# Self-attention: the weighting of a period in two halves of 256 columns, one behind each of the first two scores

## What is computed

```python
def _mha(q_in, kv_in, in_w, in_b, out_w, out_b):
    ...
    scores = jnp.einsum('bhqd,bhkd->bhqk', q, k) / jnp.sqrt(jnp.float32(dh))
    attn = jax.nn.softmax(scores, axis=-1)
    out = jnp.einsum('bhqk,bhkd->bhqd', attn, v)
    out = out.transpose(0, 2, 1, 3).reshape(q_in.shape[0], q_in.shape[1], D)
    return out @ out_w.T + out_b
...
q = _ln(latents, sa_ln_g, sa_ln_b)
x = latents + _mha(q, q, sa_in_w, sa_in_b, sa_out_w, sa_out_b)
```

## Time and profile before

| | |
|---|---|
| median of three runs | 1690.89 us |
| profiled execution | 1686.37 us, span of the trace 1684.6 us |
| TensorE busy in the span | 1441.5 us (86%) |
| VectorE busy in the span | 1181.5 us (70%) |
| ACT busy in the span | 844.1 us (50%) |
| self-attention, first to last score | 173 to 818 us |

### The profile page before, as it was taken

One profiled execution on the slowest core, in us unless ns is written; L12 is line 12 of the kernel. 1 busy time (PEld: TensorE's weight loads), 2 busy tenths in 40 slices (PEclk: granted clock), 3 DMA queues, 4 the chain that ended last, 5 costly groups with the idle time before them and its releaser, 6 DMA issues. The chain is left out here.

```text
span 1684.6 us, 29075 instructions
## 1 busy us (share of the span) xinstructions
PE 1441.5 (86%) x9973; PEld 745.6 (44%) x9974; DVE 1181.5 (70%) x1725; ACT 844.1 (50%) x1709; POOL 743.7 (44%) x465
## 2 busy tenths in 40 slices
PE   5993999999999999999658888873299999999996
PEld 3550222222222222222233544442288888888885
DVE  4755999999999999997165777434655665655653
ACT  2330788888888888888414545340022222222221
POOL 1003999999930000000131221100158887888884
PEclk8995899999999999999876979565599999999999
DMA  3556645574522111200264665535722332333331
GB/s 119 188 212 177 163 132 153 156 215 134 157 57 84 32 32 33 84 1 2 89 142 105 163 140 98 121 73 191 297 42 55 56 55 48 53 60 54 54 57 16
DMA packets 134790, 172.68 MB, mean 103 GB/s; under 512 B 30008, under 2 KB 100089, under 8 KB 134187
## 3 DMA queue, kind: packets, MB, share of 16 engines
q1 hardware_dynamic: 107499, 119.26, 26.6%
q0 software_dynamic: 27200, 52.24, 12.9%
HBM read 102.09 MB, written 66.25 MB: 100 GB/s over the span
## 5 line engine op out<-in xcount | busy, mean ns | idle before, releaser
L1093 DVE TENSOR_REDUCE sa_half_maxs<-sa_psm 128x2 f32<-128x1024 f32 x512 | 604.7, 1221 | 49.7 <-PE sa_psm L961 41.2
L1077 ACT ACTIVATE sa_p<-sa_pss 128x512 f32<-128x512 f32 x1024 | 533.0, 603 | 89.8 <-PE sa_pss L1004 89.6
L1004 PE MATMUL sa_pss<-sa_q,sa_k 49*128 49x512 f16 x1024 | 312.2, 385 | 7.8
L1019 PE MATMUL sa_pso<-sa_p,sa_v 128*32 128x512 f32 x2048 | 273.8, 606 | 18.8 <-ACT sa_o L1055 9.4
L961 PE MATMUL sa_psm<-sa_k,sa_q 48*128 48x512 f16 x1024 | 260.9, 395 | 30.5 <-DMA sa_k<-dram_sa_qk_parts 19.2
L2295 ACT ACTIVATE moe_h<-moe_psh,moe_b 128x256 f32<-128x256 f32 x312 | 122.4, 475 | 328.4 <-PE moe_psh L2232 328.4
L1004 PEld LDWEIGHTS sa_pss<-sa_q,sa_k 49*128 49x128 f16 x1024 | 77.7, 94 | 320.2 <-ACT sa_p L1077 264.9
L1366 POOL TENSOR_TENSOR x_xb<-x_xb,early_bo 128x1024 f32<-128x1024 f32 x4 | 9.4, 2350 | 373.4 <-DMA x_xb<-in_x 373.4
L2231 PE MATMUL moe_psh<-moe_hl,w_high 128*128 128x256 f16 x624 | 171.0, 274 | 0.0
L2230 PE MATMUL moe_psh<-moe_hh,w_high 128*128 128x256 f16 x624 | 170.9, 274 | 0.0
L2232 PE MATMUL moe_psh<-moe_hh,w_low 128*128 128x256 f16 x624 | 170.9, 274 | 0.0
(11 more groups left out here) (205 smaller groups left out, 2026.2 us busy)
## 6 DMA issues: line engine op xcount, KB each, us to landing
sa_w_stage<-in_w POOLq DMA_DIRECT2D x32, 512.0 KB, 5.3
dram_sa_v<-qkv_v_sb SPq DMA_DIRECT2D x8, 1024.0 KB, 5.0
dram_sa_qk_parts<-qkv_part SPq DMA_DIRECT2D x16, 512.0 KB, 6.0
sa_v<-dram_sa_v SPq DMA_DIRECT2D x16, 512.0 KB, 6.5
dram_w_high<-sa_w_high POOLq DMA_DIRECT2D x32, 256.0 KB, 2.8
dram_w_low<-sa_w_low POOLq DMA_DIRECT2D x32, 256.0 KB, 3.6
dram_sa_raw<-sa_o SPq DMA_DIRECT2D x4, 2048.0 KB, 9.1
w_high<-dram_w_high SPq DMA_DIRECT2D x16, 512.0 KB, 14.9
```

Source lines behind the costliest of these rows:

```text
L1004: pe.matmul(ps_s[place % SBANKS][:], k_st[u][rows, j0 + j, kt * kp:(kt + 1) * kp], q_st[u][rows, j0 + j, half * HALF:(half + 1) * HALF], s ...
L1019: mm = pe.matmul(ps_o[h * VW:(h + 1) * VW, :], v_st[u][:, kt, v_at:v_at + VW], probs[n % PSLOTS][h][:], start=(kt == 0), stop=(kt == key_t ...
L1077: act.activation(probs[n % PSLOTS][h][:], ps_s[place % SBANKS][:], ACT.Exp, scale=float(DH) ** -0.5).then_inc(read, 1)
L1093: dv.tensor_reduce(half_maxs[U % 2][:, at % 2, :, c], ps_m[z][:], AX_X, ALU.max).then_inc(taken, 1)
```

## The change

The weighting of a period is issued in two parts, each over all four heads: columns 0 to 255 (`side` 0) behind score 0, as before, and columns 256 to 511 (`side` 1) behind score 1, ahead of fill B. The waits stay with side 0, the increment of `weighted` goes to the last matmul of side 1. The flag that starts an accumulation is set on side 0 of the first key tile alone, the flag that ends it on side 1 of the last. A weighting so has 16 instructions in place of eight, each of half the columns, and each weight load is made twice.

```diff
-                def weigh(n):
+                def weigh(n, side):
 
                     G, half, kt = period(n)
                     u, j0, turns = home(G)
-                    if kt == 0 and half == 0 and j0 == 0:
-                        pe.wait_ge(v_loaded[u], 16 * (turns + 1))
-                    if kt == 0 and G * 2 + half > 0:
-                        pe.wait_ge(o_taken, G * 2 + half)
-                    pe.wait_ge(read, score_place(n * HG + HG - 1) + 1)
+                    if side == 0:
+                        if kt == 0 and half == 0 and j0 == 0:
+                            pe.wait_ge(v_loaded[u], 16 * (turns + 1))
+                        if kt == 0 and G * 2 + half > 0:
+                            pe.wait_ge(o_taken, G * 2 + half)
+                        pe.wait_ge(read, score_place(n * HG + HG - 1) + 1)
+                    cols = slice(side * (HALF // 2), (side + 1) * (HALF // 2))
                     for h in range(HG):
                         v_at = (j0 * 2 + h) * VW
-                        mm = pe.matmul(ps_o[h * VW:(h + 1) * VW, :], v_st[u][:, kt, v_at:v_at + VW],
-                                       probs[n % PSLOTS][h][:], start=(kt == 0), stop=(kt == key_tiles - 1))
-                    mm.then_inc(weighted, 1)
+                        mm = pe.matmul(ps_o[h * VW:(h + 1) * VW, cols], v_st[u][:, kt, v_at:v_at + VW],
+                                       probs[n % PSLOTS][h][:, cols], start=(kt == 0 and side == 0),
+                                       stop=(kt == key_tiles - 1 and side == 1))
+                    if side == 1:
+                        mm.then_inc(weighted, 1)
...
                     advance(2 * n + lead)
                     score(n * HG)
                     if n >= LAG:
-                        weigh(n - LAG)
+                        weigh(n - LAG, 0)
                     U, i = divmod(n * HG + 1, UNIT)
                     if i == TURN_AT and U + 1 < units:
                         turn(U + 1)
                     score(n * HG + 1)
+                    if n >= LAG:
+                        weigh(n - LAG, 1)
                     advance(2 * n + 1 + lead)
                     score(n * HG + 2)
                     score(n * HG + 3)
                 for n in range(groups * per_group - LAG, groups * per_group):
-                    weigh(n)
+                    weigh(n, 0)
+                    weigh(n, 1)
```

## The result

The changed kernel takes 1738.36 us (median; 1734.29 to 1757.1), the kernel before beside it 1689.27: a ratio of 1.030 (95% interval 1.026 to 1.034), 49 us more. Forecast were 1715 us, 24 to 26 more, range 1692 to 1739. So the sign was right and the loss came out twice as large. The profiled execution took 1742.12 us; its span is 1740.3 us, 55.7 over that of before.

The account below looks back on a forecast made before the run. A TensorE-ACT loop through the exponential was taken to bound the kernel, TensorE's own order after the change. 7.7 + 4.3 + 11.8 gave 24 us: 1686.4 became 1710.4, plus 4.5 for the median, 1715 us; range 1692 to 1739.

Parts of the forecast that it names:

- What bounds the kernel now: Self-attention stage before the change: a loop of TensorE and ACT sets the 2.39 us period; VectorE alone needs 2.28.
- the loop over the exponential: Score 1, its exponential, next score 0, weighting, score 1: 2.39 us before, 1.96 us with only half a weighting inside.
- TensorE's own sum becomes the bound: TensorE's work per period without waits rises from 2.19 to 2.42 us, over the old period of 2.39.
- The second loop: Over two periods, fills wait for the reduction two before; put at 2.40 us a period, right below TensorE's sum.
- The rival in which the changes of kind are hidden: Switches between scores and weightings hidden between shorter matmuls; VectorE's 2.28 us binds, 24 us less, 1667 us; chance 0.10.
- the one with bare weight loads: A half-weighting costs 0.67 us, period 2.62, 1766 us; chance 0.11 together with halves between 0.59 and 0.67.
- The "no change" rival: VectorE is the real floor, or halves cost 0.50 to 0.53 us; 1691 to 1704 us; chance 0.13.
- The two extra waits of a unit: Per eight periods: output-bank wait 0.85 us, 0.14 more than before; turn waits 0.38 for the join of the maxima.
- The sum of 24 us: Whole added time: 7.7 us from 256 periods, 4.3 from 31 bank waits, 11.8 from 31 turns.
- The granted clock is 1.00 in the stage [...] and TensorE gets busier, so I keep it: Self-attention stage: the clock was assumed to stay at 1.00 after the change, adding no time.
- The turn's wait of 0.38 us: At the turn of the row maxima, TensorE waits 0.38 us for VectorE's join of 0.18; before, a whole weighting covered it.
- The rest is free: Extra matmuls already counted, other queues keep their order, later weighting end hidden, clock kept, nothing changes outside the stage.

Follow-up runs that it names:

- e4: Changed kernel reordered: fill A, scores 0 and 1, first half-weighting, fill B, turn, scores 2 and 3, second half; 1657.76 us, 0.981 of the kernel before.
- e1: Changed kernel with both weighting halves behind score 0, one right after the other; 1693.0 us, 1.0016 of the kernel before.
- f1: e5 with ACT's copy of the output bank moved one exponential earlier, behind that of score 1; 1688.87 us, 0.9986 of the kernel before.
- f2: e5 with GpSimd's three operations on each piece of expert weights cut into four; 1713.76 us, 1.012 of the kernel before.
- e3: Changed kernel with 14 unused fp32 matmuls added between the fills ahead of the first score; 1738.71 us, 1.031 of the kernel before.
- e5: Changed kernel with the old order (both halves behind score 0) in its first 16 periods; 1719.80 us, 1.019 of the kernel before.
- e7: Changed kernel with the changed order in the first 24 periods only, old order after; 1712.61 us, 1.0125 of the kernel before.
- e6: e5 with the turn of the row maxima moved from behind the first half-weighting to behind fill B; 1727.83 us, 1.024 of the kernel before.
- f3: e4 with GpSimd's three operations on each piece of expert weights cut into four; 1657.56 us, 0.980 of the kernel before.

## Why the prediction was right and wrong

*What bounds the kernel now*: right. VectorE at 95% was not the bound; the loop over the exponential was. e4, which shortens that loop and keeps TensorE's own sum near its old size, gains 31 us.

*TensorE's own sum becomes the bound*: right, to 0.01 us a period (2.43). The second loop, put at 2.40, is at its limit too: from 180 to 830 us the loads of a fill waited 197 times for a reduction (65.1 us in total), and the rows don't tell the two apart. The rival in which the changes of kind are hidden fell with the 0.31 and 0.57 us of the first fence, the one with bare weight loads with the same 0.57 and with e1. The "no change" rival fell with VectorE's steps of 1.29 us. That the place of the halves is the reason, and not the halves, is shown by e4: the same two halves, the same two changes of kind, all scores paired, and 2.24 us. e4 also evens out the fills, which shortens the second loop; it doesn't part the two either.

*The two extra waits of a unit*: right, 0.81 for 0.85 and 0.38 for 0.38; f1 removes the first, and its unit is 0.83 us shorter. A slip beside them changed nothing: by the prediction's own steps W1 ends 0.31 + 0.57 + 0.57 - 1.00 = 0.45 us later than W did, not some 0.3.

*The sum of 24 us*: right as the price of the order. f2 shows it alone, 23.9 us, with the clock at 1.00. That the median of 1738.36 us still lies 0.6 us inside the range of 1692 to 1739 is luck: the upper part of the range was kept for halves that cost more, and they cost what was forecast.

*"The granted clock is 1.00 in the stage [...] and TensorE gets busier, so I keep it"*: this step failed, and it is the missing half. I read the clock from 180 us on and left out that the kernel before, too, enters the stage at 0.50 and has to rise out of it (183 us). Broken up as it is, the changed order takes longer to do so: 232 us, at a cost of 20.7 us in the first three units. TensorE was busy throughout (20.00 of 20.00 us at 183 to 203), so a busy engine was no assurance. e3 and e5 show that the slow units vanish when the clock is up first; e7 shows that the rise is late but not barred, and varies.

*The turn's wait of 0.38 us*, and *"The rest is free"*: right for a join of 0.18 us, but all joins were taken to be so short, and GpSimd to have no part in the loop. The trace of before had joins of 0.96, 0.50 and 0.75 us at 187.67, 208.34 and 409.34, each begun within the first 0.6 us of a GpSimd operation. With units of 20.86 us, out of step with GpSimd's pieces, joins took up to 1.99 us and stopped TensorE for up to 2.13, and the clock fell behind one of them: together 6.8 us in the profiled execution. Lost cover is the smaller part of that: with a whole weighting ahead of it a join of 2.11 us still stopped TensorE for 1.61 (e1), and f1 lacks the cover and has no such stop. f2 shows that GpSimd's long operations are the cause: cut in four, they leave no join over 0.6 us and no fall. That the step decides whether joins meet them is read from these traces; no run moved GpSimd's rhythm to test it.

What stays open: what about the unpaired order keeps the clock down so long, why the clock falls after some stops and not after others as long, and why the part of the kernel behind the stage varies by some us from execution to execution (867.7 us from the last weighting on in the changed kernel, 864.3 before, 878.7 in e3).

## What to carry to other kernels

Splitting an operation to shorten a wait is paid in changes of kind and in lost neighbours on the in-order engine: add up that engine's own sum of a period, not only the loop that the split shortens. Placed so that the neighbours stay together, the same split gained 1.9% (e4). When a change alters the length of a period, look for other work with a rhythm of its own that waits or is waited for in it, and price the wait at its longest, not at its usual length; and where a stage begins at half clock, look at what brings the clock up, not only at what it is afterwards.

## What the runs showed of the hardware

At 0.50 of the clock TensorE was busy for all of 183 to 203 us and all but 0.3 of the next 29 and its clock didn't rise until 232; in e3, brought up first by dense matmuls, the same order held 1.00 from 181 to 362 us. Stops of TensorE came right before falls: 1.57 us before 281 (e6), 1.53 before 365 (e3), 2.55 before 391 (e4), 1.61 before 393 (e1), 2.13 before 444 (the changed kernel), 1.95 before 462 (e5). Stops of 1.59 us (up to 294.7 in the changed kernel), 1.73 (271.1 in e5) and 1.65 (308.3 in f3) were followed by no fall.

The join, a VectorE operation with two inputs from SBUF, was held up by GpSimd: 1.99 us in place of 0.17, ending 0.04 us behind a TENSOR_TENSOR of GpSimd. It isn't held for the whole length that the trace shows of every operation: under a TENSOR_SCALAR shown from 417.71 to 420.48 us the join at 419.85 took 0.18 us, and joins that were held up under one ended some 1.7 us before its shown end (188.63 for 190.34 in the kernel before). The Trainium skill, "SBUF — State Buffer", "Who interferes with whom", says that VectorE with two inputs from SBUF contends with a GpSimd instruction that reads SBUF, and that the one that comes second is blocked; the trace agrees for the TENSOR_TENSOR. The reductions, which read PSUM, showed no such delay (1.16 to 1.23 us in all 512 of the changed kernel).
